# First rows of the attention stage fetched after fewer scatters, and one set of expert copies fetched later

## The reference

```python
x = x + 0.5 * ffn(layernorm(x))       # mixture of experts
x = x + attention(layernorm(x))       # Nystrom attention, 16 heads, 64 landmarks
x = x + 0.5 * ffn(layernorm(x))       # the same weights again
# ffn(x): shared = (silu(x Sg') * (x Su')) Sd'; logits = x G'; e = argmax(logits); s = sigmoid(max(logits))
#         out = shared + (silu(s x Wg[e]') * (s x Wu[e]')) Wd[e]'        8 experts, 512 hidden
# attention: q, k, v = x Wq, x Wk, x Wv; landmarks are means over 8 tokens;
#         out = softmax(q kl') @ pinv(softmax(ql kl')) @ (softmax(ql k') @ v), six iterations of the inverse
```

## Time and profile before

| | |
|---|---|
| median of 3 runs | 1126.6 us (1123.31 to 1128.51) |
| the profiled execution | 1124.68 us, of which the span is 1122.9 us |
| TensorE busy | 1074.8 us, 96% of the span |
| VectorE, ScalarE, GpSimd busy | 731.8, 552.8, 532.7 us |
| mean granted TensorE clock | 0.991 |

### The profile page before, as it was taken

How to read it: one execution, slowest core, us unless ns; L and a number is a source line. 1 busy time by engine, 2 the same in 40 slices (tenths; PEclk the granted TensorE clock), 3 DMA queues, 4 the chain that set the end, 5 groups by cost and what they waited for, 6 DMA issues and landing times.

```text
span 1122.9 us, 29672 instructions
## 1 busy us (share of the span) xinstructions
PE 1074.8 (96%) x11326; PEld 855.7 (76%) x11327; DVE 731.8 (65%) x1379; ACT 552.8 (49%) x919; POOL 532.7 (47%) x746
## 2 busy tenths in 40 slices
PE   8999998999999899999999999989999998999996
PEld 6788887788877677777777777768888887888864
DVE  5736745676664387878878868755447565776751
ACT  4344334666654365456465555343443255666641
POOL 5720543666764472452543542326201726666662
PEclk8999999999999999999999999999999999999999
DMA  7273036222224220000000000105251062222232
GB/s 263 75 279 135 19 127 219 73 68 71 73 65 156 73 92 3 3 4 3 3 4 3 3 2 3 41 2 200 82 187 38 20 238 99 75 70 71 68 108 79
DMA packets 41204, 89.77 MB, mean 80 GB/s; under 512 B 5876, under 2 KB 30583, under 8 KB 40064
## 3 DMA queue, kind: packets, MB, share of 16 engines
q1 hardware_dynamic: 30160, 62.41, 15.6%
q0 software_dynamic: 10368, 25.19, 7.1%
q10 hardware_dynamic: 560, 0.52, 0.1%
HBM read 65.03 MB, written 26.21 MB: 81 GB/s over the span
## 4 chain that ended last, share of the span: by engine, by line
PE 74%; DVE 13%; ACT 4%; issue 4%; DMA 3%; POOL 1%; DVEq 0%; ACTq 0%; POOLq 0%; SPq 0%
PE PS L1957 14%; PE PS L1871 11%; PE PS L1971 10%; PE PS L1887 7%; PE PS L2096 3%; PE PS L1964 3%; PE PS L1802 2%; PE PS L1983 2%; PE PS L2216 2%; PE PS L2229 2%; DVE A_NM L885 2%; PE PS L1905 2%; ACT XNT L1378 2%; DVE A_NM L892 1%; PE PS L1898 1%
## 5 line engine op out<-in xcount | busy, mean ns | idle before, releaser
L1957 PE MATMUL PS<-WHL,XGH 128*128 128x512 f32 x528 | 182.9, 427 | 0.7 <-DVE WHL L746 0.7
L1705 POOL TENSOR_TENSOR A_W<-A_XC,CB 128x256 f32<-128x256 f32 x86 | 61.8, 737 | 151.1 <-DVE A_XC L990 151.0
L1971 PE MATMUL PS<-WD,XNT 128*128 x528 | 128.2, 386 | 4.2 <-DVE HSB L805 4.2
L1274 ACT ACTIVATE XNT<-PS,SCORES 128x512 f32<-128x512 f32 x72 | 49.6, 688 | 147.4 <-PE PS L1957 131.2
L1612 POOL DMA_INDIRECT X<-xs_dram,WHO x72 | 92.1, 1280 | 55.6 <-issue 28.7
L1606 POOL TENSOR_SCALAR XNT<-WD 128x128 f32<-128x128 f32 x64 | 50.7, 811 | 129.5 <-DVE WD L638 129.5
L1971 PEld LDWEIGHTS PS<-WD,XNT 128*128 128x128 f32 x528 | 96.3, 192 | 18.2 <-issue 6.5
L1957 PEld LDWEIGHTS PS<-WHL,XGH 128*128 128x128 f32 x528 | 94.2, 189 | 17.5 <-issue 1.5
L1887 PE MATMUL PS<-SDH,HHL 128*128 128x256 f32 x512 | 103.4, 286 | 2.4 <-DVE X L679 2.3
L1957 PE MATMUL PS<-WHL,XGL 128*128 128x512 f32 x264 | 104.3, 395 | 0.0
L696 DVE TENSOR_TENSOR HHL<-HSB,HHL 128x512 fp32r<-128x512 f32 x64 | 45.9, 717 | 80.5 <-ACT HHL L1235 80.5
(11 more groups left out here) (300 smaller groups left out, 2620.7 us busy)
## 6 DMA issues: line engine op xcount, KB each, us to landing
xs_dram<-WG SPq DMA_DIRECT2D x16, 512.0 KB, 3.0
WU<-in_r_up SPq DMA_DIRECT2D x2, 4096.0 KB, 15.2
shared_dram<-X SPq DMA_DIRECT2D x16, 512.0 KB, 3.1
WG<-in_r_gate SPq DMA_DIRECT2D x2, 4096.0 KB, 16.9
WD<-in_r_down SPq DMA_DIRECT2D x4, 2048.0 KB, 7.9
X<-in_x SPq DMA_DIRECT2D x7, 512.0 KB, 8.9
X<-mid_dram SPq DMA_DIRECT2D x7, 512.0 KB, 3.8
X<-in_r_gate SPq DMA_DIRECT2D x6, 512.0 KB, 3.9
```

What stands on the lines that cost most here:

```text
L1274: act.activation(B["RS"][:, u * F:(u + 1) * F], banks[1 + u % 2][:], ACT.Silu, scale=B["SCORES"][:, bass.ds(t if tile is None else tile, 1 ...
L1705: pool.tensor_tensor(B["W"][:].rearrange("p (a m) -> p a m", m=M)[:, part, :], B["XC"][b % 2][:].rearrange("p (a w) -> p a w", w=XW)[:, pa ...
L1957: ins = pe.matmul(banks[bank][:], tok, w[:, k * F:(k + 1) * F], start=(k == 0 and i == 0), stop=(k == KD - 1 and i == 2))
L1971: ins = pe.matmul(banks[7][:, 0:D], B["HT"][:, u * F + f * P:u * F + (f + 1) * P], B["WD"][:, bass.ds(ex * (KF * D) + f * D, D)], start=(f ...
```

## The change

1. **First rows.** VectorE's `slot_places` of the first FFN also reduces the tile numbers of the first 512 tokens to a maximum per partition; TensorE turns that column after slot 22 (`TURN_LAST_SLOT`), VectorE reduces it to the last tile number in slot 23 (`first_rounds`), counts how many round starts are not above it and stores 16 x (that count + 1) beside the experts. SyncE waits for `ru` of position 34, reads the number, waits for that many rounds of scatters, and loads the first group in two pieces of two quarters. It waits for all scatters only ahead of the second group. ScalarE and (in the first FFN) GpSimd no longer wait for them.
2. **Entry of attention.** `selections` moves behind VectorE's half of the rows; GpSimd's memsets move behind its half of the rows and the first low weight; ScalarE begins with a square root of a constant, waits for the last down product, and takes the square root of the deviations after two of the four high weights.
3. **Second copies.** SyncE waits for nine down products (`ry_ready`) before it copies the second experts' weights of the first pair, in both FFNs.
4. **Routing.** `find_experts` moves from slot 27 to slot 26, in both FFNs.

```diff
+def round_starts():
+    whole = UNR * np.arange(1, SLOT_TILES // UNR - UNR + 1)
+    halved = whole[-1] + (UNR - 1) * np.arange(1, UNR)
+    return np.concatenate([whole, halved])
...
+    TURN_LAST_SLOT = 22
...
-                        tile_hot=22, owners=23, scores=24, read_table=27)
+                        tile_hot=22, owners=23, scores=24, find_experts=26, read_table=27)
...
             need(sp, "x_out_last", 16 * (NG - PARTS_G))
+            need(sp, "ry_ready", UNR * UNR)
             for i in range(UNR):
...
         def load_residual():
+            sp.wait_ge(s["ru"], SLOT_TILES - 1)
+            sp.wait_ge(s["rt"], FFN_PER["rt"])
+            first = sp.value_load(fb0["EXPERT"][0:1, ENTRIES:ENTRIES + 1], min_val=16, max_val=16 * TILES3)
+            for u in range(UNR):
+                sp.wait_ge(s[f"ry_out{u}"], first)
+            for j in range(0, GT, 2):
+                sp.dma_start(X3[:, j:j + 2, :], mid_rows[:, j:j + 2, :]).then_inc(s_x[j], 16)
             for u in range(UNR):
                 sp.wait_ge(s[f"ry_out{u}"], FFN_PER[f"ry_out{u}"])
...
-            for j in range(0, GT, 2):
-                sp.dma_start(X3[:, j:j + 1, :], mid_rows[:, j:j + 1, :]).then_inc(s_x[j], 16)
-            for j in range(GT):
-                sp.wait_ge(s_x[j], 32)
             load(1)
...
                 then(dve.tensor_copy(B["STILEF"], B["STILE"][:]))
+                if n == 0:
+                    then(dve.tensor_reduce(B["VM"][:, 0:1], B["STILEF"][:, 0:GT], AX_X, ALU.max))
+            def first_rounds():
+                need(dve, "cnt_ready", 3)
+                last, rounds = B["VM"][0:1, 1:2], B["VM"][0:1, 2:2 + NROUNDS]
+                then(dve.tensor_reduce(last, banks[4][0:1, 3 * P:4 * P], AX_X, ALU.max))
+                then(dve.tensor_scalar(rounds, const("round_starts", 1), last, None, ALU.is_le))
+                then(dve.tensor_reduce(last, rounds, AX_X, ALU.add))
+                dve.tensor_scalar(B["EXPERT"][0:1, ENTRIES:ENTRIES + 1], last, 16.0, 16.0, ALU.mult, ALU.add).then_inc(s["rt"], 1)
...
-            selections()
             batch_stats(0)
             batch_aggregate(0)
             first_scale()
...
+            selections()
             low_tokens(0, 0)
...
-            for u in range(UNR):
-                act.wait_ge(s[f"ry_out{u}"], FFN_PER[f"ry_out{u}"])
-            for j in range(1, GT, 2):
-                act.dma_start(X3[:, j:j + 1, :], mid_rows[:, j:j + 1, :]).then_inc(s_x[j], 16)
-            act.wait_ge(s_zero, 3)
-            for high, w in (("WQH", WQ), ("WKH", WK), ("WVH", WV), ("WOH", WO)):
+            act.activation(RSTD[:, 0:1], const("eps"), ACT.Sqrt)
+            act.wait_ge(s["ry_ready"], SLOT_TILES)
+            act.wait_ge(s_attn_w, 16 * 5)
+            weights_high("WQH", WQ)
+            weights_high("WKH", WK)
             first_deviation_of_batches()
+            weights_high("WVH", WV)
+            weights_high("WOH", WO)
...
+            batch_normalise(0)
             low_weights(0)
-            batch_normalise(0)
+            pool.memset(B["DSEL"][:], 0.0).then_inc(s_zero, 1)
...
+                if slot == TURN_LAST_SLOT and n == 0:
+                    need(pe, "rt", LAST_TILE_STEP)
+                    pe.transpose(banks[4][0:1, 3 * P:4 * P], B["VM"][:, 0:1], ident).then_inc(s["cnt_ready"], 1)
```

More of the change, by code:

```diff
@@ L59 @@
           ("pick_rows", 4), ("sel_rows", 2), ("den_rows", H),
-          ("expert_rank", E), ("tile_edges", NT), ("tile_no", SLOT_TILES), ("entry_ends", 2 * ENTRIES), ("token_next", NT), ("eps", 1)]
+          ("expert_rank", E), ("tile_edges", NT), ("tile_no", SLOT_TILES), ("entry_ends", 2 * ENTRIES), ("round_starts", SLOT_TILES // UNR - 1), ("token_next", NT), ("eps", 1)]
 CONST_AT = {}
@@ L86, in constants @@
     full = np.arange(FULL_TILES)
+    c["round_starts"][:] = round_starts()
     c["entry_ends"][:, 0::2] = np.concatenate([full, FULL_TILES + np.arange(PAIRED) // 2])
@@ L166, in emit @@
     FFN_PER = dict(stat=NT, mv=NT, seed=1 + 18, root=6 * ROOT_OPS, xn0=GT, xn=GT * (NG - 1), xt_ready=NG, xt_sb=KD * NG, lg_ready=NG // QG, lgt_sb=NG // QG, logits=NG // QG, mx=1, oh=1,
-                   act_small=2, xs_out=16 * NG, cnt_ready=2, rt=37, slots=1, rows_hot=NT // 4, cols_hot=2, table=1, who=3, expert_of=1, nobody=2,
+                   act_small=2, xs_out=16 * NG, cnt_ready=3, rt=42, slots=1, rows_hot=NT // 4, cols_hot=2, table=1, who=3, expert_of=1, nobody=2,
                    gu=KF * NG, silu=KF * NG, h=KF * NG, x_new=2 * NG, gath0=16 * TILES3, gath1=16 * TILES3,
@@ L190, in emit @@
     assert sorted(tile_at(p) for p in range(SLOT_TILES)) == list(range(SLOT_TILES)) and FIRST_HALVED % UNR == 0
+    for m in range(SLOT_TILES):
+        rounds = int((round_starts() <= m).sum())
+        assert rounds == SLOT_TILES // UNR - 1 or all(p // UNR <= rounds for p in range(SLOT_TILES) if tile_at(p) <= m)
     GIVEN = {"xs_out", "h", "x_new", "ry"}
@@ L206, in emit @@
     GATE_BANK, UP_BANK = (0, 5), (1, 6)
+    NROUNDS = TILES3 - 1
+    LAST_TILE_STEP = 35
     def root_of(n, g):
@@ L238, in ffn_buffers @@
                  STILE=b("STILE", NT, I32), SROW=b("SROW", NT, I32), EXF=b("EXF", ENTRIES),
-                 EXPERT=b("EXPERT", ENTRIES, I32), WHO=b("WHO", SLOT_TILES, I32), SCORES=b("SCORES", SLOT_TILES))
+                 EXPERT=b("EXPERT", ENTRIES + 1, I32), WHO=b("WHO", SLOT_TILES, I32), SCORES=b("SCORES", SLOT_TILES))
         B["XNT"], B["XS"] = XNT, X[:, NT * D:]
@@ L639, in slot_places @@
                 then(dve.tensor_copy(B["STILEF"], B["STILE"][:]))
+                if n == 0:
+                    then(dve.tensor_reduce(B["VM"][:, 0:1], B["STILEF"][:, 0:GT], AX_X, ALU.max))
+                    assert step[0] == LAST_TILE_STEP
+            def first_rounds():
[5 more added lines that the diff above has]
+                dve.tensor_scalar(B["EXPERT"][0:1, ENTRIES:ENTRIES + 1], last, 16.0, 16.0, ALU.mult, ALU.add).then_inc(s["rt"], 1)
+                step[0] += 1
             cols = B["COLS"].rearrange("p (v t c) -> p v t c", v=2, t=NT)
@@ L671, in find_experts @@
                 then(dve.tensor_reduce(B["EXF"][:], past.rearrange("p (t w) -> p t w", w=2 * E), AX_X, ALU.add))
-                dve.tensor_scalar(B["EXPERT"][:], B["EXF"][:], float(-E), float(E - 1), ALU.add, ALU.min).then_inc(s["expert_of"], 1)
+                dve.tensor_scalar(B["EXPERT"][:, 0:ENTRIES], B["EXF"][:], float(-E), float(E - 1), ALU.add, ALU.min).then_inc(s["expert_of"], 1)
             def shared_out(g):
@@ L731, in shared_group @@
                     elif slot == ROUTING_SLOT["owners"]:
+                        if n == 0:
+                            first_rounds()
                         owners()
@@ L734, in shared_group @@
                         scores()
+                    elif slot == ROUTING_SLOT["find_experts"]:
+                        find_experts()
                     elif slot == ROUTING_SLOT["read_table"]:
-                        find_experts()
                         read_table()
@@ L740, in ffn_vector @@
                 shared_group(g)
-            assert step[0] == FFN_PER["rt"]
+            assert n == 1 or step[0] == FFN_PER["rt"]
             def low_weights(w, ex, i, slot):
@@ L834, in batch_stats @@
                 for j in range(GT):
-                    if g == 0:
+                    if g == 0 and j % 2 == 0:
                         dve.wait_ge(s_x[j], 32)
@@ L1403, in product_kept, with weights_high @@
                              banks[c][:, 0:PC * HS].rearrange("p (a d) -> p a d", d=HS)).then_inc(att["tp"], 1)
-            for u in range(UNR):
-                act.wait_ge(s[f"ry_out{u}"], FFN_PER[f"ry_out{u}"])
-            for j in range(1, GT, 2):
-                act.dma_start(X3[:, j:j + 1, :], mid_rows[:, j:j + 1, :]).then_inc(s_x[j], 16)
-            act.wait_ge(s_zero, 3)
-            for high, w in (("WQH", WQ), ("WKH", WK), ("WVH", WV), ("WOH", WO)):
+            def weights_high(high, w):
                 act.copy(B[high][:], w).then_inc(s_high, 1)
@@ L1649, in ffn_pool @@
                     gather_residual(ahead, ahead % UNR)
-            for u in range(UNR):
-                pool.wait_ge(s[f"ry_out{u}"], (n + 1) * FFN_PER[f"ry_out{u}"])
+            if n == 1:
+                for u in range(UNR):
+                    pool.wait_ge(s[f"ry_out{u}"], (n + 1) * FFN_PER[f"ry_out{u}"])
         def attention_pool():
@@ L1727, in low_outputs @@
                     pool.tensor_tensor(B["OTL"][:, part], B["OT"][:, part], B["OTH"][:, part].bitcast(F32), ALU.subtract).then_inc(att["otl"], 1)
+            batch_normalise(0)
             low_weights(0)
-            batch_normalise(0)
+            pool.memset(B["DSEL"][:], 0.0).then_inc(s_zero, 1)
+            pool.memset(B["NM1"][:], 0.0).then_inc(s_zero, 1)
+            pool.memset(B["NM3"][:], 0.0).then_inc(s_zero, 1)
             for i in range(1, 4):
```

3 lines of the change are left out of this document (removed).

## The result

The changed kernel takes 1115.47 us (median of 6 runs, 1114.5 to 1120.75) against 1126.26 beside it (6 runs): ratio 0.9916, 95% interval 0.989 to 0.9942, so 6.5 to 12.4 us faster. (A ratio is taken over all runs and can differ from the quotient of the medians by about 0.001.) The profiled execution took 1114.59 us, its span 1112.8, the mean granted clock 0.995.

The account below looks back on a forecast made before the run. TensorE, busy 96% of the span, was taken as the bound, so gains come from its gaps: 3.5 + 5.0 + 1.1 - 0.8 + 0 = 8.8, forecasting 1117.8 us against the median of 1126.6; range 1112.5 to 1123.5.

Parts of the forecast that it names:

- First routed phase: First FFN's routed start: without copies beside it the residual gather lands sooner; gain 5.0 us, bounds 3.0 and 5.7.
- The gap of the turn: First FFN's routed start: TensorE's idle 1.36 ahead of a turn stays or goes; 0 to 1.4 gained, 0.9 taken.
- Second routed phase: Second FFN's routed start: only the gather's excess transfer, 3.85 - 2.8, leaves the gap of 1.71; gain 1.1 us.
- The 2.98: Second FFN: time without named cause before the gather's issue; if the copies caused it, both gaps go: 3.6 us.
- More: Rival: the 2.98 and both second-FFN gaps go, and the turn's gap in the first: gain 12.4, 1114.2 us; 10%.
- Tile nine: Near the ninth tile, where the copies land: a 3.8 gather stalls TensorE 0.4 per FFN; -0.8 in all.
- The copies' harm moves with them: Rival: ninth-tile gathers take as long as the first did; gain 0 to 3 us, 1124.5; 12%.
- the worst row: Ninth tile: a gather of 7.13, 4.3 over, would stall TensorE 3.7 and cost 6.7 us per FFN.
- Entry: Attention's entry: early first rows let the turns start right behind the keep-busy matmuls; gain 3.5 us, bounds 2.4 and 4.2.
- selections waits for the memsets until 381.6 and needs 0.9: Attention's entry: VectorE's selections, at 0.9 us after the memsets, are done before VectorE is next wanted at 385.1.
- The clock's share: Attention's entry: turns at full clock take 1.10 for 1.93; ScalarE's first copy starts 0.7 after them instead of 1.1.
- Routing: Added reduction and turn, VectorE's small operations and find_experts one slot earlier: together 0 us, bounds -1 and +1.

Follow-up runs that it names:

- experiment 1: Kernel before plus only the second copies' wait for nine down products: 1120.72 us, ratio 0.9968 to the kernel before.
- experiment 7: Changed kernel with the gather of tile five issued ahead of the first scatter: 1112.02 us, ratio 0.9858 to the kernel before.
- Experiment 8: Changed kernel with the second copies behind three down products for nine, in both FFNs: 1117.4 us, ratio 0.9908 to the kernel before.
- experiment 3: Changed kernel with six keep-busy matmuls for sixteen ahead of attention's entry: 1119.31 us, ratio 0.9946 to the kernel before.
- experiment 4: Changed kernel with the first group's rows again waiting for all scatters, reordered entry kept: 1124.4 us, ratio 0.9996 to the kernel before.
- experiments 5 to 9: Changed kernel with entry recut, six keep-busy matmuls (0.9859) or sixteen (0.9901); early tile-five gather (0.9858); copies behind three products (0.9908); six-matmul recut plus early gather (0.987).
- experiments 5 and 6: Changed kernel with attention's entry recut (selections earlier, low weights awaited in pairs), with six or sixteen keep-busy matmuls: 1112.5 us (0.9859) and 1117.62 us (0.9901).
- the run with sixteen: Changed kernel with attention's entry recut and all 16 keep-busy matmuls kept: 1117.62 us, ratio 0.9901 to the kernel before.

## Why the prediction was right

**First routed phase: 5.0, measured 4.4** (4.4 in experiment 1 as well). The gather fell below 4.5 and the product runs at full clock, as said. The gap of the turn was taken to shrink by 0.9, and shrank by 0.4: GpSimd's queue makes it, as experiment 7 showed. I took that gap to move with both its sides, and did not ask which order of issue made it.

**Second routed phase: 1.1, measured 1.1.** Only the transfer's excess went. The 2.98 stayed with the copies gone, so they were not its cause, and the rival *More* fell with it. What the 2.98 is stays open.

**Tile nine: -0.4 for each FFN, measured -0.2 in the first and -0.5 in the second.** The turn waited 0.23 and 0.59. Experiment 8 shows that the fear behind *The copies' harm moves with them* was sound in kind: 2.4 more for a gather beside the copies, less than the 4.3 of the worst row. The reason against it was read wrongly: the gather of 3.8 in the earlier trace rows was issued at 325.12, 11 us ahead of the 1 MB of copies at 336.36, so it was not in their company. That rival's sum is off as well: 9.6 - 6.7 less 1.0 to 3 is at most 1.9, not 3.

**Entry: 3.5, measured 3.6.** The early rows came as worked out (their loads are issued at 360.53, 10.8 ahead of the statistics), and the turns started behind the last keep-busy record at 9.17 from the first, for 9.2. The size holds, but two of the steps behind it fail.

- *"selections waits for the memsets until 381.6 and needs 0.9"*. It waits until 377.39 and then takes 4.9, because its copies run beside GpSimd's subtractions: 1.35 each for 0.29. The prediction took the duration from a row in which GpSimd stood idle and moved it to a place where GpSimd is busy. That it cost nothing is luck, for it was hidden with nothing to spare: the low parts are ready at 382.65 (382.31 + 0.34 in the chain), TensorE's products ahead end at 382.58 (382.19 + 0.39), and its product with the low parts starts at 382.70. Experiments 3 and 4 lift one cover each, and both show TensorE waiting for this chain, for 4.4 and 4.5.
- *The clock's share.* I counted 0.8 for turns at the full clock and 0.4 for a first copy that starts sooner behind them. In experiment 1 the turns took 1.09 with the old order, and the next projection started 3.72 behind them, against 4.06 in the kernel before, behind a wait for the fourth low weight:

```profile
385.94 0.50 PE L2097 MATMUL PS<-A_XTH,A_WQH 128*128 128x512 f32 x1 [0.34 <-POOL A_WOL L1722]
```

So the clock was worth 0.3 of the 3.6. Turns that start earlier brought 2.8 (from -3.74 to -6.49: 386.54 against 380.05), and 0.5 more came from GpSimd's low weights, no longer the last to end: after the change the next projection starts 3.2 behind the turns (383.27 - 380.05).

The Trainium skill, "SBUF — State Buffer", section "SBUF: two separate sides", states the rule that I passed over: VectorE and GpSimd share one pair of SBUF ports under a lock. A VectorE instruction takes it in a two-port mode, or with two inputs in SBUF while GpSimd reads SBUF; whichever engine starts first keeps the pair for its whole instruction, and the other waits. The traces agree: the copies start 1.27 apart, in step with GpSimd's subtractions (1.25 apart), and fall to 0.2 apart where GpSimd computes nothing. That the ports are what binds them was not tested by itself.

**Routing: 0, measured -0.1**, the added turn (from +0.61 to +0.69 behind slot 22); it showed no wait. By 183 us the difference is down to +0.39; whether the move of `find_experts` did that was not tested by itself.

**The rest.** The start of the program lost 0.6, and had done so by 60 us, ahead of every edit. Between 740 and 752 us 1.3 were gained with no edit near. The windows of the kernel before there:

```profile
748.00:750.00 2.00, 1.29 (x6) 1.32 (x7) 1.46 (x4) 1.12 (x3) 1.15 (x2) 0.61 0.00 0
750.00:752.00 2.00, 2.00 (x12) 1.52 (x15) 0.27 (x1) 0.07 (x1) 0.00 (x0) 0.54 0.04 8
```

Both traces of the changed kernel show 1.00 there. So 1.3 of the profiled 10.1 is a dip that one execution had and another had not. Another 0.6 came inside attention. By the edits' own steps the gain is 4.4 + 3.6 + 1.1 - 0.1 - 0.2 - 0.5 (tile nine, twice) = 8.3, for 8.8 forecast; the medians' 10.8 has an interval from 6.5 to 12.4, and does not tell the two apart.

## What to carry to other kernels

A duration belongs to the company in which it was measured: before moving an operation, look at what the other engines do at its new place, and price it by a row from such a place. When a chain gets shorter, list the next two bounds, since lifting one alone gained nothing here and lifting both gained 4.4 at its place. A bulk copy beside a gather lengthens it each time, by 0.6 to 4.3 us (0.6, 1.05, 1.2, 2.4, 3.3 and 4.3 over the 2.8 of an undisturbed gather), and what the kernel pays is that less the gather's slack: read both at the place to which the copy moves. Look at GpSimd's order of issue before blaming the transfer.

## What was unexpected of the hardware

- VectorE's copies of 128x256 take 0.23 to 0.29 with GpSimd idle and 1.35 beside its subtractions.
- An idle stretch is followed by the lower clock in one execution and not in the next. Idle 1.96 at the entry of the kernel before was, 1.85 in experiment 1 wasn't; in the second FFN 1.97 in experiment 1 was (the product took 3.53), 1.88 in the kernel before wasn't. The length doesn't decide it: ahead of that same turn, 1.89 in experiment 4 was (3.40), and 1.97 in experiment 3 wasn't:

```profile
932.89 0.44 PE L1941 MATMUL PS<-CB,X 128*128 128x128 f32 x2 [1.97 <-DMA X<-xs_dram,WHO]
933.16 1.92 PE L2010 MATMUL PS<-WD,XNT 128*128 x8
```

  Of the traces of experiments 5 to 9, three have one such dip in attention, each at another place and each worth 1.7 (what the windows lack to 1.00, times their length). In the run of experiment 8, whose attention is the changed kernel's own:

```profile
516.00:518.00 2.00, 0.93 (x49) 0.67 (x37) 0.06 (x1) 0.80 (x2) 0.00 (x0) 1.00 0.03 8
518.00:520.00 2.00, 1.31 (x19) 0.83 (x23) 0.74 (x2) 0.76 (x2) 0.00 (x0) 0.92 0.00 0
520.00:522.00 2.00, 2.00 (x36) 0.94 (x32) 1.20 (x4) 0.92 (x2) 0.88 (x1) 0.50 0.03 8
```

  In the run with sixteen of experiments 5 and 6, TensorE is as little busy there (0.86 of 2.00 at 516) and the clock stays at 1.00. The difference inside attention moves at the full clock too: from -0.01 at 480 us to +2.6 at 600 between the run with sixteen and the changed kernel. A difference of 1 to 3 us between two single traces is therefore no proof of an edit; its step in the timeline, at the edit's own place, is.
- A gap of 0.97 without a named cause ahead of a turn in one trace of the changed kernel stood ahead of the down product behind it in the other (0.79). That product starts at 193.07 and at 192.99: the gap moves by itself, and the loss stays.
